# Shared row fetches for tile 13 and the last tile, and layer 3 in front of the fifth group, in a deep-and-cross ranker

## The reference

```python
x0 = emb[ids].reshape(ids.shape[0], -1)
x = x0
for i in range(cross_w.shape[0]):          # 3 cross layers
    s = x @ cross_w[i]
    x = x0 * s[:, None] + cross_b[i] + x
h = jax.nn.relu(x0 @ w1 + b1)              # 1664 -> 1024
h = jax.nn.relu(h @ w2 + b2)               # 1024 -> 512
h = jax.nn.relu(h @ w3 + b3)               # 512 -> 256
logit = jnp.concatenate([x, h], axis=1) @ out_w + out_b
return jax.nn.sigmoid(logit)
```

## Time and profile before

| | us |
|---|---|
| three executions, median | 513.7 |
| the profiled execution's own time | 512.91 |
| its span, from the first to the last instruction | 511.1 |
| PE busy | 478.2 (94%) |
| weight loads on PE | 441.8 (86%) |
| POOL busy | 369.2 (72%) |
| DVE busy | 263.3 (52%) |
| ACT busy | 26.3 (5%) |
| PE waiting at its transposes of x for DVE | 16.6, in 15 waits |

### The profile page before, as it was taken

How to read it: one execution, slowest core, us unless ns; L and a number is a source line. 1 busy time by engine, 2 the same in 40 slices (tenths; PEclk the granted TensorE clock), 3 DMA queues, 4 the chain that set the end, 5 groups by cost and what they waited for, 6 DMA issues and landing times.

```text
span 511.1 us, 14003 instructions
## 1 busy us (share of the span) xinstructions
PE 478.2 (94%) x2912; PEld 441.8 (86%) x2912; DVE 263.3 (52%) x610; ACT 26.3 (5%) x42; POOL 369.2 (72%) x397
## 2 busy tenths in 40 slices
PE   2599899999998999999999998999999999999997
PEld 1399798999998898989889897888989998899996
DVE  5667555545453545535454552645544554545435
ACT  4542000000000000000000000000000000000012
POOL 5777777777777777777777777777777777777730
PEclk9999999999999999999999999999999999999999
DMA  8981111111111111111111111111111111111100
GB/s 240 386 287 29 30 27 29 27 30 29 29 27 30 28 29 28 28 30 27 28 27 31 28 27 29 30 27 29 26 29 30 27 28 27 31 28 28 28 17 1
DMA packets 18270, 24.59 MB, mean 48 GB/s; under 512 B 8013, under 2 KB 9000, under 8 KB 18184
## 3 DMA queue, kind: packets, MB, share of 16 engines
q0 software_dynamic: 12480, 12.80, 13.2%
q1 hardware_dynamic: 4186, 9.71, 5.3%
q10 hardware_dynamic: 1518, 1.18, 0.7%
HBM read 24.41 MB, written 0.01 MB: 48 GB/s over the span
## 4 chain that ended last, share of the span: by engine, by line
PE 71%; POOL 12%; issue 7%; DMA 6%; DVE 2%; ACT 0%; DVEq 0%; POOLq 0%
PE l_bank L739 55%; POOL x_raw L361 12%; DMA x_raw<-in_L_rec_emb,idx 6%; PE x_bank L739 4%; PE x_bank L751 4%; PE h_bank L793 3%; PE h_bank L835 1%; PE l_bank L824 1%; DVE x_raw L505 1%; PE h_bank L763 1%; DMA ids<-in_r_ids 1%; PE h_bank L739 1%; PE l_bank L763 0%; DVE h1T_lo L534 0%; DVE h1T_hi L516 0%
## 5 line engine op out<-in xcount | busy, mean ns | idle before, releaser
L361 POOL DMA_INDIRECT x_raw<-in_L_rec_emb,idx x390 | 368.4, 945 | 121.3 <-issue 100.9
L739 PE MATMUL l_bank<-w_hi,xT_hi 128*128 128x342 f32 (+1 forms) x624 | 145.4, 333 | 0.0
L739 PE MATMUL l_bank<-w_lo,xT_hi 128*128 128x342 f32 (+1 forms) x624 | 137.7, 321 | 0.0
L739 PE MATMUL l_bank<-w_hi,xT_lo 128*128 128x342 f32 (+1 forms) x624 | 137.5, 320 | 0.0
L739 PEld LDWEIGHTS l_bank<-w_lo,xT_hi 128*128 128x128 f32 x624 | 106.6, 190 | 0.0
L739 PEld LDWEIGHTS l_bank<-w_hi,xT_lo 128*128 128x128 f32 x624 | 106.0, 189 | 0.0
L739 PEld LDWEIGHTS l_bank<-w_hi,xT_hi 128*128 128x128 f32 x624 | 103.6, 190 | 2.3
L512 DVE CAST xT_hi<-x_bank 128x256 fp32r<-128x256 f32 (+1 forms) x86 | 38.5, 448 | 96.5 <-PE x_bank L751 96.5
L505 DVE COPY_PREDICATED x_raw<-past,x_bank 128x256 f32<-128x256 int32 (+3 forms) x96 | 44.7, 466 | 41.8 <-DMA x_raw<-in_L_rec_emb,idx 40.2
L751 PE MATMUL x_bank<-identity,x_raw 128*128 128x128 f32 x208 | 39.5, 278 | 16.7 <-DVE x_raw L505 16.6
L739 PE MATMUL l_bank<-w_hi,h1T_hi 128*128 128x512 f32 x120 | 48.7, 406 | 1.0 <-DVE h1T_lo L534 1.0
(11 more groups left out here) (98 smaller groups left out, 319.5 us busy)
## 6 DMA issues: line engine op xcount, KB each, us to landing
ids<-in_L_rec_emb SPq DMA_DIRECT2D x1792, 0.2 KB
ids<-in_L_rec_emb ACTq DMA_DIRECT2D x1536, 0.2 KB
w_raw<-in_L_rec_w SPq DMA_DIRECT2D x18, 512.0 KB, 12.9
x_raw<-in_L_rec_emb,idx POOLq DMA_INDIRECT x390, 2.4
b_rows<-in_L_rec_b ACTq DMA_DIRECT2D x1, 512.0 KB, 7.3
b_rows<-in_L_rec_b ACTq DMA_DIRECT2D x1, 256.0 KB, 8.5
ids<-in_r_ids SPq DMA_DIRECT2D x1, 207.0 KB, 2.6
b_rows<-in_L_rec_b ACTq DMA_DIRECT2D x1, 128.0 KB, 9.0
```

What stands on the lines that cost most here:

```text
L361: pool.indirect_dma_start(out=dst, out_offset=None, in_=emb, in_offset=rows).then_inc(landed, 16)
L739: done = pe.matmul(bank[:, 0:b - a], x[:, k, :], w[:, k, a:b], start=(k == 0 and n == 0), stop=(k == last_k and n == 2))
```

## The change

Who fetches what, and when:

- SP no longer fetches for the last tile as it does for the others; it has three buffers instead of four. ACT no longer fetches field 20 of the last tile, and has three buffers instead of two.
- Three fields are *shared*: field 24 of tile 13, and fields 23 and 25 of the last tile. SP fetches the first 56 or 64 samples' rows, ACT the others, straight into `x_raw` and without a copy by DVE. Both wait until tile t-2 has been transposed there. They stand behind the rows of tile 13 in both queues, and behind those of tile 14. POOL gathers field 20 of the last tile, and neither of the others.
- SP issues ten loads of weights and goes on to rows; ACT issues the other eight between its roundings of tile 0, and in tile 0 it fetches 4, 8, 4 and 16 rows in front of its four roundings of x.

The order of the layers:

- Layer 3 of tile t-1 stands in front of the transposes of tile t's fifth group, in `h_bank[1]`; DVE's part follows the fifth group's remainder.
- h1 is transposed and split in four quarters over four banks (the two `h_bank` and the two `x_bank`), and DVE copies the dots behind it instead of in front.

```diff
-    SP_TILES = list(range(2, TILES))
+    SP_TILES = list(range(2, TILES - 1))
-    SP_BUFS = 4
-    ACT_TILES = [2, 3, 5, 6, 7, 8, 10, 11, 12, 13, 14, 15]
+    SP_BUFS = 3
+    ACT_TILES = [2, 3, 5, 6, 7, 8, 10, 11, 12, 13, 14]
-    ACT_BUFS = 2
-    ACT_FIRST = 16
+    ACT_BUFS = 3
+    ACT_FIRST = [4, 8, 4, 16]
+    SHARED = [(TILES - 3, GROUPS[-1][-1] * FPK, 56), (TILES - 1, LAST_GROUPS[-1][-1] * FPK + 1, 64), (TILES - 1, LAST_GROUPS[-2][-1] * FPK + 1, 64)]
...
-        return not (t in SP_TILES and f == sp_field(t) or t in ACT_TILES and f == ACT_FIELD)
+        return not (t in SP_TILES and f == SP_FIELD or t in ACT_TILES and f == ACT_FIELD or (t, f) in [s[:2] for s in SHARED])
...
+    SP_LOADS = 10
+    ACT_LOADS = 14
...
+        def shared_free(t, f):
+
+            return seen(t - 2) + next(g for g, ks in enumerate(groups(t - 2)) if f // FPK in ks) + 1
...
             for i, t in enumerate(SP_TILES):
                 if i >= SP_BUFS:
                     sync.wait_ge(sp_placed, i - SP_BUFS + 1)
+                fetch(SP_FIELD, t, 0, P, sp_rows[i % SP_BUFS], sp_landed[i % SP_BUFS])
+                for i, (u, f, cut_at) in enumerate(SHARED):
+                    if u == t or t == SP_TILES[-1] and u > t:
+                        sync.wait_ge(x_transposed, shared_free(u, f))
+                        fetch(f, u, 0, cut_at, x_buf[u % 2][:, f * E:(f + 1) * E], shared_landed[i])
...
+            def fetch_shared(i):
+                t, f, cut_at = SHARED[i]
+                act.wait_ge(x_transposed, shared_free(t, f))
+                for p in range(cut_at, P, ACT_REGS):
+                    regs = [act.alloc_register(f"act_row_shared{i}_{p + j}") for j in range(min(ACT_REGS, P - p))]
+                    row = AT_ROWS.index((f, t))
+                    act.load(regs, at_bytes[row:row + 1, p:p + len(regs)])
...
+                        if n == 2:
+                            load_weights(range(SP_LOADS, ACT_LOADS))
+                            act.wait_ge(sp_idx_ready, 1)
+                            fetch(ACT_FIRST[0])
+                    if g == 0:
+                        load_weights(range(ACT_LOADS, len(LOADS)))
                     if g == 1:
                         load_rows()
-                    if g == len(FIRST_GROUPS) - 1:
-                        act.wait_ge(sp_idx_ready, 1)
-                        fetch(ACT_FIRST)
+                    if g > 0:
+                        fetch(ACT_FIRST[g])
                     x_hi(0, g)
-                fetch(ACT_REGS - ACT_FIRST)
-                while fetched[0] < P * len(ACT_TILES):
-                    fetch(ACT_REGS)
+                for j, t in enumerate(ACT_TILES):
+                    while fetched[0] < P * (j + 1):
+                        fetch(ACT_REGS)
+                    for i, (u, _, _) in enumerate(SHARED):
+                        if u == t or t == ACT_TILES[-1] and u > t:
+                            fetch_shared(i)
...
             def h1_lo(t):
-                for half in range(2):
+                for q in range(QUARTERS):
+                    h1_hi(t, q)
...
                     if g == 3:
                         h2_lo(t - 1)
+                    if g == 4:
+                        l3_out(t - 1)
                 l1_out(t)
+                h1_lo(t)
                 dots_out(t)
-                h1_lo(t)
-                l3_out(t - 1)
...
                 for g in range(1, NG):
                     l1(t, g, slice(0, -ahead(t)))
+                    if g == 3:
+                        l3(t - 1)
                     if g < NG - 1:
                         transpose_x(t, g + 1)
                     l1(t, g, slice(-ahead(t), None))
                 transpose_h1(t)
-                l3(t - 1)
```

More of the change, by code:

```diff
@@ L217, in parts, with weights @@
             return [w[:, k:k + m, 0:WIDTH // m] for w in of]
+        def weights(n):
+            name, k, m = LOADS[n]
+            return {"w1": w1, "w2": w2, "w3": w3}[name][k * P:(k + m) * P, :].rearrange("(m p) c -> p m c", m=m)
+        def shared_free(t, f):
+            return seen(t - 2) + next(g for g, ks in enumerate(groups(t - 2)) if f // FPK in ks) + 1
         def half_of(part, i):
@@ L267, in dcn_ranker_kernel @@
         act_placed = sem("act_placed")
+        shared_landed = [sem(f"shared_landed{i}") for i in range(len(SHARED))]
         xT_hi_ready = sem("xT_hi_ready")
@@ L294, in _, with fetch @@
             sync.dma_start(ids[:, QUICK:TILES * F], r_ids.rearrange("(p t) f -> p (t f)", p=P)[:, QUICK:TILES * F]).then_inc(ids_loaded, 16)
-            for n, (name, k, m) in enumerate(LOADS):
-                src = {"w1": w1, "w2": w2, "w3": w3}[name][k * P:(k + m) * P, :].rearrange("(m p) c -> p m c", m=m)
-                sync.dma_start(parts(n)[0], src).then_inc(weights_loaded[n], 16)
+            for n in range(SP_LOADS):
+                sync.dma_start(parts(n)[0], weights(n)).then_inc(weights_loaded[n], 16)
             sync.wait_ge(sp_idx_ready, 1)
+            def fetch(f, t, a, b, rows, landed):
+                for p in range(a, b, SP_REGS):
+                    regs = [sync.alloc_register(f"sp_row{f}_{t}_{p + j}") for j in range(min(SP_REGS, b - p))]
+                    row = AT_ROWS.index((f, t))
+                    sync.load(regs, at_bytes[row:row + 1, p:p + len(regs)])
+                    for j, reg in enumerate(regs):
+                        at = sync.snap(reg, donate=True, min_val=0, max_val=(2 * H - 1) * ROW)
+                        sync.dma_start(rows[p + j:p + j + 1, :].bitcast(U8), emb_bytes[:, bass.DynSlice(at, ROW)],
+                                       bounds_check="skip_entire_dma").then_inc(landed, 16)
             for i, t in enumerate(SP_TILES):
@@ L500, in make_whole @@
                                                              for f in fields(groups(u)[g])))
-                if t in SP_TILES and sp_field(t) in range(a, a + n):
+                if t in SP_TILES and SP_FIELD in range(a, a + n):
                     dve.wait_ge(sp_placed, SP_TILES.index(t) + 1)
@@ L504, in make_whole @@
                     dve.wait_ge(act_placed, ACT_TILES.index(t) + 1)
+                for i, (u, f, _) in enumerate(SHARED):
+                    if u == t and f in range(a, a + n):
+                        dve.wait_ge(shared_landed[i], 16 * P)
                 dve.copy_predicated(x_buf[t % 2][:, a * E:(a + n) * E].rearrange("p (f e) -> p f e", e=E),
@@ L799, in transpose_h1 @@
                     pe.wait_ge(h2T_ready, t)
-                for half in range(2):
-                    h1_chunks(t, h_bank[half], range(half * HB, (half + 1) * HB))
+                    pe.wait_ge(h3_ready, t)
+                for q, bank in enumerate(H1_BANK):
+                    h1_chunks(t, bank, range(q * QB, (q + 1) * QB))
             def transpose_h1_last(t):
                 pe.wait_ge(h3_ready, t)
-                for q, bank in enumerate(H1_LAST):
+                for q, bank in enumerate(H1_BANK):
                     h1_chunks(t, bank, range(q * QB, (q + 1) * QB))
             def l2(t, ks):
-                pe.wait_ge(h1T_ready, 2 * t + 1 + ks[-1] // HB)
                 if t == 0:
@@ L849, in l3 @@
                 for k in ks:
[L850 removed]
+                    done = three_passes([(l3_bank, 0, N3)], h2T_hi, h2T_lo, w3_hi, w3_lo, k, K3 - 1)
                 if k == K3 - 1:
```

71 lines of the change are left out of this document (35 added, 36 removed).

## The result

| | before | changed |
|---|---|---|
| runs, median (lowest to highest) | 513.79 us (512.95 to 513.92, 4 runs) | 529.25 us (528.8 to 530.04, 4 runs) |
| ratio, 95% interval | | 1.0303, 1.029 to 1.0316 |
| profiled execution | 512.91 us, span 511.1 | 528.86 us, span 527.1 |

The change costs 3.0%. I had forecast 522.7 us in a range of 519.2 to 526.0: the sign and the path of the delay came as forecast, the size did not.

The account below looks back on a forecast made before the run. POOL's gathers paced the tiles, PE the last tile's end; ACT's later rows would now delay it. 6.9 (late rounding) + 2.1 (slow pace) + 0 = +9.0 us: 521.9, carried onto the median 522.7 us, range 519.2 to 526.

Parts of the forecast that it names:

- Rows on ACT: ACT's single-row queue: added rows at 0.21 us each, less a buffer wait, move its last row from 481.2 to 490.3.
- +6.9: Last tile's third group: PE starts its matmuls at 491.2 instead of 484.33, because ACT's rounding stands behind its rows.
- Chain from ACT's last row to the end: Last tile: rounding 0.05 us after the last row, remainder 0.42 later, PE 0.47 behind, then 26.8 us without waits.
- Pace after standing still: PE after a stall of some 8 us runs at half clock for a while: +2.1 us, bounds 0 and 4.
- rival 2: The stall comes without the slow pace; PE goes on at 0.48 us a triple: 520.6 us. Chance 15%.
- Start: Tile 0: moved weight loads and early rows delay ACT's fourth rounding by 0, bounds 0 and 3 us.
- Rival 3: ACT's weight loads and early rows delay tile 0's fourth rounding by 3 us or more: 525.7 and up. Chance 9%.
- Rows on SP: SP's row queue: last row out at 488.6, hidden because PE needs those fields well behind 491.
- POOL: 389 gathers instead of 390; those from the end of tile 13 come 1.25 us sooner, worth nothing while ACT holds PE.
- Layer part: Layer 3 before the fifth group, h1 in quarters: a tile of PE alone gets 0.7 us longer, hidden; bounds 0 to -1.3.
- Rival 1: ACT's rows are done in time and POOL's lost gather sets the end: 512.4 us. Chance 6%.

Follow-up runs that it names:

- matmuls in the stall: Changed kernel plus 60 extra unread matmuls of 512 columns on PE in the last tile, in front of the third group's layer 1: 527.04 us, ratio 1.0254.
- (field 24): Changed kernel, but the third shared field is field 24 of the last tile instead of 25: 522.14 us, ratio 1.0157.
- field 25 skipped: Changed kernel with the last tile's 128 field 25 addresses moved past the table's end, so none of its rows is fetched: 519.92 us, ratio 1.0121.
- the version with DVE's roundings: Changed kernel, but all roundings of x in the last tile go to DVE; field 25 stays shared: 523.33 us, ratio 1.0187.
- the kernel before with SP's field 25: Kernel before, but SP fetches field 25 of the last tile in place of 23, which POOL gathers; nothing shared: 526.43 us, ratio 1.0237.

## Why the prediction was wrong, point by point

**The step that failed** is the price of a row, "which leaves 6.8 for the 32 rows, 0.21 for one", which "Rows on ACT" uses for every row of the change. The count of 1608 rows held, and there was no wait for a buffer and no delay from the start. But 64 of ACT's new rows are of field 25 and cost 0.33 each. The last two blocks, load and rows, take 12.8 and 13.0 us instead of 8.97, which is +7.9. They begin 0.8 us sooner than forecast, at 471.6, by a smaller miss the other way: the short block in tile 13, taken at 3.9 us, took 2.7, since its load of 8 addresses is quicker than one of 32. So the last row leaves at 497.4, not 490.3, a miss of 7.1. The time missed by 529.25 - 522.7 = 6.6. The term "+6.9" of the sum measured +14.0.

The hint was in my own rows: the earlier trace rows has 90/90/524 for 1520 rows of the kernel before, and a median of 90 ns for a DMA of 256 bytes was not asked what it does. The code line has `bounds_check`, and the packets of the queue in any short stretch would have shown that most of these DMAs move nothing.

**Chain from ACT's last row to the end**: right. Rounding at once, remainder 0.42 us later, PE 0.48 behind that, no further wait.

**Pace after standing still**: forecast 2.1, measured 5.29 - 3.21 = 2.1, and 2.2 came back with the matmuls in the stall. My lowest bound 0 and rival 2 (15%) are out, and so is the bound of 4 for a slow stretch as long as the stall. The stall was nearly twice as long as forecast, and the price about the same: 2.1 us behind 13.95, 2.3 behind 7.62 (field 24), 1.7 behind 5.29 (field 25 skipped).

**Start**: right at 0. Rival 3 is out, though the changed time lies in its stretch of the axis; it had the place wrong.

**Rows on SP**: the same miss, forecast 488.6 and out near 497.8. "Hidden" was right only because ACT was as late; the version with DVE's roundings shows it unhidden, 7.74 us.

**POOL**: 389 gathers as forecast, but the last starts at 490.48 where 489.05 was forecast. 3 ns more for each of 389 are 1.2 us, as much as the lost gather saves. These 3 ns don't belong to the change: the version with matmuls in the stall has the same fetches, 945 ns and its last gather at 489.48, and the kernel before with SP's field 25 has 390 gathers of 947 ns and the last at 491.44. Among the profiles at one pace (945 or 947 ns) the last gather starts 0.3 to 1.4 us sooner with 389 gathers than with 390. So the lost gather is there, and the pace differs by as much from one profile to the next; why, was not tested.

**Layer part**: a tile of PE alone was forecast 28.45 + 0.7 = 29.15 and reads 29.17 us. It lay in the stall. Tile 14's last transposes were forecast at 462.6 and came at 464.05: PE, at 29.2 us a tile, had become the bound by then. Part of this may be the half clock in tile 9, told at the end, which the forecast didn't have: in the version with matmuls in the stall, whose profile is without it and whose gathers are quicker, the same transposes start at 463.01.

**Rival 1** did not come: ACT was not done in time. Even with ACT off the path and a field that is mostly skipped, the change is at 0.9989, 513.29 us, and not at the rival's 512.4. That gain is hardly above what can be told, and that it is POOL's lost gather was not shown.

## What to carry to other kernels

A price per row read from a trace holds for the data of that trace: where a DMA can be skipped, read its shortest, median and longest time and the packets of the queue, and ask of a new field how many of its rows are real. Put no compute step on the critical path behind a queue that issues single rows, since every row's price then counts for the end. A stall on TensorE costs its length and, here, about 2 us of slow pace behind it, whether it was 5 or 14 us long.

## What the hardware showed that I had not expected

- A skipped row is not free: it keeps ACT's queue 90 ns and SP's 73, a fetched one 228 on either. With what stands around it, a row in a block of ACT costs 0.18 us skipped and 0.33 fetched.
- Registers are loaded at a price for each. ACT's address loads in the changed kernel, first one of 4 addresses, then, in tile 0, one of 8 and one of 4, one of 16 together with the first of 32, then 32 full ones, and last the seven of the shared fields, one of them of 8:

```profile
L434 ACTq TENSOR_LOAD <-at_bytes x1: 508/508/508, 12.4 to 12.4; - x1
...
L434 ACTq TENSOR_LOAD <-at_bytes x2: 325/538/752, 30.2 to 33.1; - x2
...
L434 ACTq TENSOR_LOAD <-at_bytes x2: 1037/1594/2152, 39.4 to 47.2; - x2
...
L434 ACTq TENSOR_LOAD <-at_bytes x32: 2144/2188/2298, 47.2 to 326.0; - x32
...
L420 ACTq TENSOR_LOAD <-at_bytes x7: 741/2199/2305, 397.6 to 484.4; - x7
```

 0.33 and 0.51 us for 4, 0.74 and 0.75 for 8, 1.04 for 16, 2.19 for 32. I had taken 2.2 for every load.
- A wait of 1.97 us in tile 9 of the changed kernel was followed by the half clock, one of 1.77 at the same place before was not. Granted clock of the changed kernel:

```profile
315.00:319.00 4.00, 3.70 (x15) 3.73 (x16) 1.00 (x3) 0.00 (x0) 2.93 (x4) 0.57 0.11 25
```

 and of the kernel before:

```profile
315.00:319.00 4.00, 4.00 (x27) 4.00 (x26) 0.39 (x1) 0.00 (x0) 2.97 (x4) 1.00 0.14 26
```

 Of the other versions, field 25 skipped has a wait of 1.86 us there and the half clock behind it, and the one with field 25 and the last tile's roundings on DVE has 1.88 us and keeps the full clock. Granted clock of the first, then of the second:

```profile
315.00:319.00 4.00, 4.00 (x17) 4.00 (x16) 0.85 (x2) 0.00 (x0) 3.08 (x4) 0.57 0.13 26
```

```profile
315.00:319.00 4.00, 4.00 (x28) 4.00 (x27) 0.77 (x2) 0.00 (x0) 3.04 (x4) 1.00 0.15 25
```

 So the length of the wait alone doesn't decide it. I had held waits of this size harmless; what decides was not tested.
